# The position-bias network of two attention layers: sigmoid by hyperbolic tangent, layer-norm scales on the transposed side, 512-column blocks

## What is computed

```python
def ln(x, g, eps=1e-05):
    mean = x.mean(axis=-1, keepdims=True)
    var = ((x - mean) ** 2).mean(axis=-1, keepdims=True)
    return (x - mean) * jax.lax.rsqrt(var + eps) * g

def rel_pos_bias(n, w0, b0, g0, w1, b1, g1, w2, b2, dtype):
    pos = jnp.arange(-n + 1, n, dtype=dtype)[:, None]
    h = jax.nn.silu(ln(pos @ w0 + b0, g0))
    h = jax.nn.silu(ln(h @ w1 + b1, g1))
    h = h @ w2 + b2
    ...
```

```python
sim = jnp.einsum('bhid,bjd->bhij', q, k) * SCALE
bias = rel_pos_bias(n, w0, b0, g0, w1, b1, g1, w2, b2, q.dtype)
```

## Time and profile before

| | |
|---|---|
| median of 3 runs | 2514.55 us (2511.8 to 2519.36) |
| the profiled execution, its own time | 2516.95 us |
| its span, first to last instruction | 2514.8 us |
| busy in the span | PE 2031.9 us, DVE 1753.7, ACT 1335.7, POOL 1144.4 |
| granted TensorE clock, mean | 0.907 of full speed |

### The profile page before, as it was taken

One profiled execution on the slowest core, in us unless ns is written; L12 is line 12 of the kernel. 1 busy time (PEld: TensorE's weight loads), 2 busy tenths in 40 slices (PEclk: granted clock), 3 DMA queues, 4 the chain that ended last, 5 costly groups with the idle time before them and its releaser, 6 DMA issues. The chain is left out here.

```text
span 2514.8 us, 46901 instructions
## 1 busy us (share of the span) xinstructions
PE 2031.9 (81%) x11738; PEld 1439.0 (57%) x11738; DVE 1753.7 (70%) x4112; ACT 1335.7 (53%) x2872; POOL 1144.4 (46%) x1544
## 2 busy tenths in 40 slices
PE   6993287799999988678888888885277699999988
PEld 5883254566666657465555556554155466666657
DVE  5877855688878855656666666646946688887865
ACT  2221255577766653355566556542245577777753
POOL 1221104566766632026666666622103566666642
PEclk8997588899999999789998999997588799999999
DMA  2001046433333331476676666641045543333323
GB/s 72 25 14 39 3 166 216 153 106 113 101 119 116 101 110 62 165 257 185 207 210 200 197 197 198 195 168 39 1 135 192 184 127 100 116 103 112 122 93 109
DMA packets 171006, 322.41 MB, mean 128 GB/s; under 512 B 22838, under 2 KB 51132, under 8 KB 170844
## 3 DMA queue, kind: packets, MB, share of 16 engines
q1 hardware_dynamic: 170844, 320.59, 40.7%
HBM read 242.76 MB, written 94.52 MB: 134 GB/s over the span
## 5 line engine op out<-in xcount | busy, mean ns | idle before, releaser
L1358 POOL TENSOR_SCALAR at_row<-at_row,at_inv 128x129 f32<-128x129 f32 (+7 forms) x384 | 725.3, 1889 | 306.4 <-DVE at_inv L1515 303.9
L1562 ACT ACTIVATE at_row<-at_row,at_nmax 128x129 f32<-128x129 f32 (+7 forms) x768 | 595.2, 775 | 217.4 <-DVE at_nmax L1534 214.5
L1534 DVE CUSTOM_DVE_ANT_0 at_row<-at_s,bias,at_row 128x128 f32<-128x128 f32 (+7 forms) x768 | 623.2, 811 | 109.5 <-PE at_s L1462 50.8
L1474 PE MATMUL at_t<-ident,at_row 128*128 128x128 f32 x3456 | 551.1, 288 | 113.5 <-POOL at_row L1358 81.4
L1474 PEld LDWEIGHTS at_t<-ident,at_row 128*128 128x128 f32 x3456 | 400.6, 145 | 312.8 <-POOL at_row L1358 145.7
L1461 PE MATMUL at_s<-k_hh,q_hl 128*128 128x512 f32 (+3 forms) x1152 | 466.7, 405 | 48.3 <-SPq L1424 32.0
L1490 PE MATMUL at_o<-at_pt,v 128*64 128x512 f32 (+3 forms) x2304 | 443.5, 508 | 7.9 <-ACT at_pt L1555 6.2
L1555 ACT ACTIVATE at_pt<-at_t 128x512 f32<-128x512 f32 (+2 forms) x576 | 309.0, 536 | 226.0 <-PE at_t L1474 219.6
L1373 DVE COPY at_pt<-at_t 128x128 f32<-128x128 f32 (+3 forms) x576 | 278.9, 484 | 194.6 <-PE at_t L1474 193.2
L1462 PE MATMUL at_s<-k_lp,q_h 65*128 65x512 f32 (+3 forms) x1152 | 395.9, 356 | 0.0
L1461 PEld LDWEIGHTS at_s<-k_hh,q_hl 128*128 128x128 f32 x1152 | 228.4, 198 | 89.9 <-SPq L1424 33.4
(11 more groups left out here) (223 smaller groups left out, 3088.4 us busy)
## 6 DMA issues: line engine op xcount, KB each, us to landing
q_hl<-q_dram SPq DMA_DIRECT2D x192, 256.0 KB, 4.4
bias<-bands_dram SPq DMA_DIRECT2D x64, 512.0 KB, 5.6
q_dram<-pj_qh SPq DMA_DIRECT2D x96, 256.0 KB, 2.4
q_dram<-pj_ql SPq DMA_DIRECT2D x96, 256.0 KB, 2.3
q_h<-q_dram SPq DMA_DIRECT2D x96, 256.0 KB, 5.1
o_dram<-at_o_sb SPq DMA_DIRECT2D x96, 256.0 KB, 4.5
o_in<-o_dram SPq DMA_DIRECT2D x12, 2048.0 KB, 8.8
bands_dram<-brow_dram SPq DMA_DIRECT2D x2, 8192.0 KB, 32.6
```

The lines of the kernel that those rows point to most:

```text
L1358: return eng.tensor_scalar(cells, cells, inv[:, i:i + 1], None, ALU.mult)
L1474: last = eng.transpose(t_ps[m % NTR][:, c * P:(c + 1) * P], row[:, u % RING, here:here + P], t["ident"][:])
L1534: eng.tensor_tensor_reduce(out=row[:, u % RING, ZERO:ZERO + width], in0=s_ps[u % 2][:, 0:width], in1=bt[:, lo:lo + width], scale=-1.0, sca ...
L1562: eng.activation(cells, cells, ACT.Exp, scale=-1.0, bias=nmax[:, i:i + 1], accum_out=rsum[:, i:i + 1]).then_inc(s["exp"], 1)
```

## The change

The network is written anew, with the same inputs and the same result `rb_brow`. With z the normalized value before its scale g, silu(g z) = (g/2) z (1 + tanh(g z / 2)).

- Normalization moves to ScalarE: VectorE makes `rstd` and `off = -mean * rstd` (4 columns each), and ScalarE computes `z = rstd * h + off`, one instruction of 128x256 for each tile, with both as operands per row.
- z is transposed unscaled, 8 transposes for a half, into PSUM buffers of 4 banks in all. On the transposed side a column is a row, so that g/2 is one number per partition: ScalarE computes `th = tanh(half_g * z)` from PSUM on 128x512, VectorE `u = (th + 1) * z` (one instruction, 128x512), ScalarE rounds it, VectorE takes the low part.
- The factor g/2 that is left is put into the weights of the next product: `split_weights` multiplies `w1` and `w2` by it before they are split. It now stands behind the first layer's statistics, where the split of the weights stood ahead of everything.
- `exp`, `1 + e`, its reciprocal of 128x1024, the two multiplications of 128x1024 and the scale are gone. The scales g0 and g1 are loaded as 128x2 (1 KB) and not as rows spread over 128 partitions (128 KB each). TensorE has the same matmuls, with 16 transposes for each layer as before.
- In the second hidden layer VectorE does `null_columns` ahead of the two last silu parts instead of behind them, and finishes one half (bias, statistics, offset) before it begins the other.

The diff, cut to its core; the old `distance_layer` and the old lists of ScalarE and TensorE, which it removes whole, stand with the kernel above:

```diff
-            vec = {n: sb(f"rb_{n}", [P, D]) for n in ("w0", "b0", "g0", "b1", "g1")}
+            vec = {n: sb(f"rb_{n}", [P, D]) for n in ("w0", "b0", "b1")}
+            g = [sb(f"rb_g{n}", [P, KD]) for n in range(NS)]
             w1 = sb("rb_w1", [P, KD, D])
             w1h, w1l = (sb(f"rb_w1{n}", [P, KD, D], FR) for n in "hl")
             w2 = sb("rb_w2", [P, KD, P])
             w2h, w2l = (sb(f"rb_w2{n}", [P, KD, P], FR) for n in "hl")
             b2 = sb("rb_b2", [H, 1])
             h = sb("rb_h", [P, NT, D])
-            e = sb("rb_e", [P, NT, D])
+            z = sb("rb_z", [P, NT, D])
             stats = sb("rb_stats", [P, NT, 6])
             mv = sb("rb_mv", [P, NT, 2])
-            rstd = sb("rb_rstd", [P, NT])
-            hth, htl = (sb(f"rb_ht{n}", [P, KD, S], FR) for n in "hl")
+            rstd, off = (sb(f"rb_{n}", [P, NT]) for n in ("rstd", "off"))
+            half_g = sb("rb_half_g", [P, NS, KD])
+            th, u = (sb(f"rb_{n}", [P, KD, S]) for n in ("th", "u"))
+            uh, ul = (sb(f"rb_u{n}", [P, KD, S], FR) for n in "hl")
             brow = sb("rb_brow", [H, BROW])
-            tr = [ps(f"rb_tr{n}", [P, BANK])[:, 0:KD * P] for n in range(2)]
+            tr = [ps(f"rb_tr{n}", [P, KD, BANK]) for n in range(NT // HALF)]
             mm = ps("rb_mm", [P, NT, D])
...
+                    for n in range(NS):
+                        load("rb_in", g[n][:], w[f"g{n}"])
...
+                def distances(i):
+                    for n in range(i * HALF, (i + 1) * HALF):
+                        last = eng.scalar_tensor_tensor(h[:, n, :], vec["w0"][:], t["dist"][:, n:n + 1], vec["b0"][:],
+                                                        ALU.mult, ALU.add)
+                    rb.step(last)
+
+                def add_first_bias(i):
+                    eng.wait_ge(s["mm"], i + 1)
+                    rb.step(eng.tensor_tensor(h[:, tiles(i), :], mm[:, tiles(i), :],
+                                              vec["b1"][:].unsqueeze(1).to_broadcast([P, HALF, D]), ALU.add))
+
+                def variances(m):
+                    at = tiles(m % 2)
+                    rb.settle()
+                    for n in range(at.start, at.stop):
+                        last = eng.bn_stats(stats[:, n, :], h[:, n, :])
+                    rb.step(last)
+                    rb.settle()
+                    for n in range(at.start, at.stop):
+                        last = eng.bn_aggr(mv[:, n, :], stats[:, n, :])
+                    rb.step(last)
+                    rb.settle()
+                    eng.tensor_scalar(rstd[:, at], mv[:, at, 1], EPS, None, ALU.add).then_inc(s["var"], 1)
+
+                def offsets(m):
+                    at = tiles(m % 2)
+                    eng.wait_ge(s["std"], m + 1)
+                    rb.step(eng.reciprocal(rstd[:, at], rstd[:, at]))
+                    rb.settle()
+                    eng.scalar_tensor_tensor(off[:, at], mv[:, at, 0], -1.0, rstd[:, at], ALU.mult, ALU.mult
+                                             ).then_inc(s["offset"], 1)
+
+                def silu(m):
+                    for kk in range(KD):
+                        eng.wait_ge(s["tanh"], KD * m + kk + 1)
+                        eng.scalar_tensor_tensor(u[:, kk, cols(m)], th[:, kk, cols(m)], 1.0, tr[m % 2][:, kk, :],
+                                                 ALU.add, ALU.mult).then_inc(s["silu"], 1)
+
+                def low_silu(m):
+                    for kk in range(KD):
+                        eng.wait_ge(s["high"], KD * m + kk + 1)
+                        eng.tensor_tensor(ul[:, kk, cols(m)], u[:, kk, cols(m)], f32(uh[:, kk, cols(m)]), ALU.subtract
+                                          ).then_inc(s["low"], 1)
+
+                def split_weights():
+                    for layer, x in ((0, w1), (1, w2)):
+                        for kk in range(KD):
+                            last = eng.tensor_scalar(x[:, kk, :], x[:, kk, :], g[layer][:, kk:kk + 1], 0.5, ALU.mult, ALU.mult)
+                    rb.step(last)
+                    rb.settle()
+                    for full, hi in ((w1, w1h), (w2, w2h)):
+                        last = eng.tensor_copy(hi[:], full[:])
+                    rb.step(last)
+                    rb.settle()
+                    for full, hi, lo in ((w1, w1h, w1l), (w2, w2h, w2l)):
+                        eng.tensor_tensor(lo[:], full[:], f32(hi[:]), ALU.subtract).then_inc(s["w_split"], 1)
...
-                for full, hi in ((w1, w1h), (w2, w2h)):
-                    rb.step(eng.tensor_copy(hi[:], full[:]))
-                rb.settle()
-                for full, hi, lo in ((w1, w1h, w1l), (w2, w2h, w2l)):
-                    rb.step(eng.tensor_tensor(lo[:], full[:], f32(hi[:]), ALU.subtract))
-                distance_layer(0)
+                distances(0)
+                variances(0)
+                distances(1)
+                variances(1)
+                offsets(0)
+                offsets(1)
+                split_weights()
+                silu(0)
+                low_silu(0)
+                silu(1)
+                low_silu(1)
                 null_key()
-                distance_layer(1)
+                for i in range(2):
+                    add_first_bias(i)
+                    variances(2 + i)
+                    offsets(2 + i)
                 null_columns()
-                eng.wait_ge(s["mm"], len(HALVES) + 1)
+                for i in range(2):
+                    silu(2 + i)
+                    low_silu(2 + i)
+                eng.wait_ge(s["mm"], 3)
...
+                def deviation(m):
+                    eng.wait_ge(s["var"], m + 1)
+                    eng.activation(rstd[:, tiles(m % 2)], rstd[:, tiles(m % 2)], ACT.Sqrt).then_inc(s["std"], 1)
+
+                def normalize(m):
+                    at = tiles(m % 2)
+                    eng.wait_ge(s["offset"], m + 1)
+                    if m >= 2:
+                        eng.wait_ge(s["tr"], m - 1)
+                    for n in range(at.start, at.stop):
+                        last = eng.activation(z[:, n, :], h[:, n, :], ACT.Identity, scale=rstd[:, n:n + 1], bias=off[:, n:n + 1])
+                    last.then_inc(s["normal"], 1)
+
+                def tangent(m):
+                    eng.wait_ge(s["tr"], m + 1)
+                    if m == 0:
+                        eng.wait_ge(s["rb_in"], 16 * 9)
+                    if m >= 2:
+                        eng.wait_ge(s["silu"], KD * (m - 1))
+                    for kk in range(KD):
+                        eng.activation(th[:, kk, cols(m)], tr[m % 2][:, kk, :], ACT.Tanh, scale=half_g[:, m // 2, kk:kk + 1]
+                                       ).then_inc(s["tanh"], 1)
+
+                def high_silu(m):
+                    if m >= 2:
+                        eng.wait_ge(s["mm"], m - 1)
+                    for kk in range(KD):
+                        eng.wait_ge(s["silu"], KD * m + kk + 1)
+                        eng.activation(uh[:, kk, cols(m)], u[:, kk, cols(m)], ACT.Copy).then_inc(s["high"], 1)
+
+                eng.wait_ge(s["rb_in"], 16 * 9)
+                for n in range(NS):
+                    last = eng.activation(half_g[:, n, :], g[n][:], ACT.Copy, scale=0.5)
+                last.then_inc(s["half"], 1)
+                eng.wait_ge(s["half"], 1)
+                deviation(0)
+                deviation(1)
+                normalize(0)
+                normalize(1)
+                tangent(0)
+                high_silu(0)
+                tangent(1)
+                high_silu(1)
+                fold()
+                deviation(2)
+                deviation(3)
+                normalize(2)
+                normalize(3)
+                tangent(2)
+                high_silu(2)
+                tangent(3)
+                high_silu(3)
...
+                def transposes(m):
+                    eng.wait_ge(s["normal"], m + 1)
+                    if m >= 2:
+                        eng.wait_ge(s["silu"], KD * (m - 1))
+                    for kk in range(KD):
+                        for n in range(HALF):
+                            last = eng.transpose(tr[m % 2][:, kk, n * P:(n + 1) * P],
+                                                 z[:, m % 2 * HALF + n, kk * P:(kk + 1) * P], t["ident"][:])
+                    last.then_inc(s["tr"], 1)
+
+                def second(m):
+                    eng.wait_ge(s["w_split"], 1)
+                    eng.wait_ge(s["low"], KD * (m + 1))
+                    for n in range(m * HALF, (m + 1) * HALF):
+                        for kk in range(KD):
+                            last = three_products(eng, mm[:, n, :], [x[:, kk, n * P:(n + 1) * P] for x in (uh, ul)],
+                                                  [x[:, kk, :] for x in (w1h, w1l)], kk == 0, kk == KD - 1)
+                    last.then_inc(s["mm"], 1)
+
+                transposes(0)
+                transposes(1)
+                second(0)
+                second(1)
```

(13 more changed lines are left out.)

90 lines of the change are left out of this document (5 added, 85 removed).

## The result

The changed kernel takes 2434.89 us, median of 4 runs (2430.04 to 2441.57); the kernel before took 2513.18 in the runs beside them (2506.56 to 2519.36). The ratio is 0.9691, with a 95% interval of 0.9653 to 0.9728: 78 us less. A second comparison, later, gave 0.9697 (0.9684 to 0.9711).

A forecast was written before the change was run, and what follows sets the result against it. VectorE's chain with its reciprocals bounds the preparations: 85.4 and 86.3 us become 49.7 each, saving 35.7 and 36.6, plus 2 x 1.0 for loads, 74.3 together. From the median 2514.55 that predicts 2440 us, range 2428 to 2454.

The forecast's parts named there:

- a slow tangent: Rival: tangent costs what VectorE's reciprocal does on 128x512, 3353 ns; 43 us back, 2483 us; chance 0.03.
- no effect: Rival: the change does nothing, only if the reciprocals were not on the path; chance 0.02.
- null key done: Preparation, between the two hidden layers: VectorE's null key takes 3.7 us as before, so the second layer begins at 23.3.
- Normalization: ScalarE, eight of 128x256 in a preparation: 0.61 us each, 2.2 for four with overlap; bounds -1.0 to +0.6 for eight.
- Tangent, u, high, low: ScalarE and VectorE by turns on 128x512: 0.69, 0.74, 0.63, 0.69 us, pipelined; a layer's low parts end at +6.3.
- Table load: ScalarE, before the tangents: 1.28 us on the path, no drain; rival: costs more, 2445 us, by the skill's page 2446; chance 0.12.
- The hold by GpSimd: Second layer's statistics: VectorE's L723 waits until GpSimd ends at 34.0; rival: no hold, 3 us shorter each, 2434; chance 0.08.
- Cover: Weights' split lies under the first half's normalization and transposes, else up to 3.3 us; null columns lie in VectorE's wait.
- Last products: End of a preparation: six of 12 products after the last low part take 2.1 us; 1.6 upper clock, 2.7 lower.
- the loads: Before each preparation: two 128 KB rows become 1 KB; landing earlier by 0 to 2 us, taken as 1.0.
- Nothing else in the program changes: Sum of the forecast: only the preparations and loads of layers 1 and 3 give time, together 74.3 us.
- The rival with the clock in attention: Both attention phases: shorter rest lowers TensorE's clock; gain eaten at about a tenth of work, 2532 us at 12%; chance 0.02.

The follow-up runs named there:

- The tangent alone: Kernel before, own layout, with tanh(h/2) for exp(-h) and 0.5 (e + 1) for 1 + e and its reciprocal: 2460.98 us, ratio 0.9775.
- the doubled tangents: Changed kernel with every tangent computed twice, the first into a tile nobody reads: 2446.1 us in one run.
- the pieces: Changed kernel with GpSimd's null products and low part of the query weights in pieces of 512 columns, 4 and 4 instructions for 2 and 1: 2429.51 us.
- without its cover: Changed kernel with the weights' scaling and split moved ahead of the first statistics: 2438.42 us in one run.
- The two experiments with loads: Changed kernel with row b1 loaded three times over in one 384 KB transfer, 2446.11 us; or with two more 128 KB loads, 2445.23 us.
- the changed kernel's second one: Second profile of the unaltered changed kernel, from its rerun beside the shared normalization on one chip: median 2431.68 us, ratio 0.9697.
- the layout: Changed kernel with exponential, 1 + e, reciprocal and product on the transposed side in place of the tangent: 2504.12 us, ratio 0.9951.
- the seven writes: Changed kernel with seven unread tiny writes more in VectorE's list, ahead of its wait for the loads in layers 1 and 3: 2440.71 us, ratio 0.9716.
- the shared version: Changed kernel with each layer's second half normalized by VectorE and the null columns split: 2424.07 us, ratio 0.9646; again 2431.12 us, ratio 0.9699.

## Why the prediction was right

**What bounded the kernel** was read rightly: the reciprocals of the earlier trace rows on VectorE. The tangent alone takes them off and gains 51.4 of the 78.3 us, nearly their 52.4 us of busy time; the rivals with a slow tangent and with no effect fall with it.

**The steps**, in us from the first operation (225.41 in the timeline of layer 1):

| step | predicted | measured |
|---|---|---|
| second square root done | 7.7 | 7.6 |
| second half normalized | 12.0 | 11.7 |
| tangent starts | 13.3 | 13.0 |
| null key done | 23.3 | 22.6 |
| GpSimd starts, ends | 24.8, 34.0 | 24.2, 33.3 |
| second layer's normalization done | 38.6 | 37.5 |
| its tangent starts | 39.9 | 38.8 |
| low parts of the first, second half | 43.5, 46.2 | 42.3, 45.0 |
| bias row done | 49.7 | 48.5 |

The eleven steps came in the order and with the waits that the prediction gave them; the chain runs a little shorter than priced:

- *Normalization*: 587 ns each, and eight take 4.04 us and not 4.3, since neighbours on ScalarE overlap by 0.1. The price of 0.61 that I drew from the scale operand was right for one alone. The bounds for both preparations should have been twice as wide, since there are 32 normalizations and not 16 (-4 to +2.4); the measured -1.0 lies inside both.
- *Tangent, u, high, low*: 0.678, 0.682, 0.630 and 0.688 us, priced 0.69, 0.74, 0.63, 0.69. The two halves of a layer take 6.2 us from the first tangent to the last low part (264.21 to 270.37), priced 6.3. One thing was misread here: the bounds count four tangents of a preparation on the path, and the doubled tangents show that all eight are (5.0 and 5.4 us for eight of 0.68). With 0.68 for 0.69 it moved nothing.
- *Table load*: no drain. The tangent follows its load by 0.02 us at 238.44 and 264.21. The rule that I weighed (the Trainium skill, "ScalarE: Activation LUTs", "What ACT_TABLE_LOAD costs") is not borne out here: the load is 1.28 us as it says, the further 1.38 isn't there. That rival falls, and so does its time of 2446.
- *The hold by GpSimd*: it stood where I put it, ended with GpSimd, and the pieces showed its cause. What I had left open, whether small operations between are held too, has its answer: two more are, for 0.7 and 1.6 us, and it costs nothing here, because the last hold ends with GpSimd in any case. The Trainium skill, "SBUF — State Buffer", "Who interferes with whom", gives a pair of ports that is locked for a whole instruction by GpSimd or by some of VectorE's operations, those with two SBUF inputs among them. The offset has two such inputs and took 1.80 us beside GpSimd where the same operation took 0.16 at 232.89, which agrees.
- *Cover*: the split of the weights was hidden (3.3 and 3.1 us without its cover, priced up to 3.3), the null columns too, between 259.29 and the tangent.
- *Last products*: 2.3 us from the last low part to the bias row, priced 2.1. They began 0.43 us apart and ended 0.22 to 0.24 apart; the granted clock of 270.40 to 272.60 is 0.72, a mean of the lower level and the upper one. The bound of +1.4 for both layers should have been +1.2, from my own 2.7 against 2.1.

**The size that was off a little is the loads.** I took 1.0 us for each layer; it was 1.1 in layer 1 and 2.1 in layer 3, just beyond the bound of 2. The two experiments with loads show that bytes move the landing; by how much isn't settled, since what 256 KB cost when added (3.6 to 4.5) is more than what they gave when taken away.

**"Nothing else in the program changes" was wrong, and one of the prediction's own signs of being wrong came true: a later phase changed its length.** Layer 1's attention is 6.7 us shorter than before in the profiles. The prediction held the later phases for untouched because their code is. The kernel before has 24 VectorE instructions more ahead of that phase; it stops in it for 1.20 us at about +74 and for 1.04 at about +132, and its stretch from the 21st to the 39th reciprocal takes 66.9 us against 63.6, so 3.3 of the 6.7 come from there. The rest isn't explained. The rival with the clock in attention falls: in the windows of these two phases the granted clock is 1.00 and 0.99, against the earlier trace rows.

```profile
421.00:886.00 465.00, 437.50 (x2680) 290.83 (x2680) 370.63 (x956) 327.04 (x736) 297.36 (x385) 1.00 0.36 108
1890.00:2355.00 465.00, 440.46 (x2688) 294.70 (x2688) 370.09 (x960) 329.76 (x741) 298.37 (x388) 0.99 0.35 108
```

So the preparations gave 78.3 where I had 74.3: 2.7 from chains shorter than priced, 1.2 from the loads. The kernel before was also 1.4 us faster in the runs beside them (2513.18) than the 2514.55 from which I started; both together, less 0.3 of rounding, are the 5.1 by which 2440 was too high. The difference of the medians, 78.3, happens to be the same as that of the preparations, and that is luck: the 8.2 outside the preparations stand in two single profiles, and the changed kernel's second one has 2.5 (its attention 1 is as short, 466.6, but layer 2's takes 3.7 more than in the first).

## What to carry over

Where an engine's expensive operation is on the path, look for the form that another engine evaluates at its usual price, and then for what that form lets you fuse: here the tangent gave 51 us, the layout 15, and both 12 more than that. Price each new form by the nearest row and add 0.1 us for each operand per partition, then lay the steps out in time from engine to engine; the eleven times above came out within 1.2 us. A change can alter the length of a phase whose code it does not touch, here by 6 to 8 us: cut the profile by phases, compare the same instruction in two kernels, and look for idle time put down to nothing, or to an engine that had long been done, before you believe a difference of 0.3%.

## What the hardware showed

**VectorE stops at fixed instructions of a phase with nothing to wait for, and how long depends on how many instructions its own list has ahead of it.** The table under the seven writes shows it. In the seven-writes kernel two packets of the queue of instructions move between 490.5 and 491.3 us, VectorE stands from 491.3 to 493.67, and another such packet moves right behind; in the shared version the same pair lies at 484 to 485 and the stop at 485.3 to 487.48. From 481.8 to 598 the shared version moves ten packets of that queue; the changed kernel, which doesn't stop there, moves none from 488.5 to 604.5. That the stops are waits for these packets is my reading, not shown: the trace doesn't say whose instructions they carry. The changed kernel has longer stops in layer 2's attention, up to 3.86 us:

```profile
1428.47 0.62 DVE L1427 TENSOR_SCALAR at_row<-at_row,at_inv 128x769 f32<-128x769 f32 x1 [3.86 <-issue]
```

They don't always cost their length. In that phase the changed kernel stops for 16.1 us in all and the shared one (again) for 6.7, and they take 557.8 and 557.3 us. The Trainium skill, "Runtime: NRT & Kernel Launch", "Instruction fetch mechanics", says that an engine's instructions come in blocks and that a crossing is mostly hidden. No run here shows that these stops are such crossings; if they are, they cost 3 to 7 us in a stretch of 63.

**A tangent on ScalarE costs little more than a copy:** 0.68 us for 128x512 with a scale per partition, against 0.63 for the rounding copy of the same shape (L846) and 3.35 for VectorE's reciprocal.

**256 KB more of small loads ahead of a phase cost 3.6 to 4.5 us**, where removing as many had saved 1.1 and 2.1.
